# The second attention's first turn made beside the mixture's last batch

## The reference

```
# layer 0, second half: a dense mixture of 8 experts
probs = softmax(x1 @ gate_w + gate_b)
h = relu(einsum('bsd,edf->bsef', x1, w1) + b1)
moe = einsum('bse,bsed->bsd', probs, einsum('bsef,efd->bsed', h, w2) + b2)
x = x + memory(xn) + layernorm(x1 + moe)             # the sum of layer 0
xn = layernorm(x)
# layer 1
qkv = xn @ Wqkv.T + b                                # 16 heads of 8
ctx = causal_attention(q, k, v)
q2 = conv1d(ctx); out = causal_attention(q2, k, v) @ out_w.T
# and, beside it, 32 routed experts, top 8 of a router on xn, with capacity 128
x = x + out + routed(xn)
```

## Time and profile before

| | |
|---|---|
| three runs | 3534.44 us median, 3531.47 to 3535.82 |
| profiled execution, its time | 3539.05 us |
| its span, first to last instruction | 3537.2 us |
| mean granted TensorE clock | 0.968 of full |
| busy PE, DVE, ACT, POOL | 91%, 73%, 59%, 24% of the span |
| DMA | 151.89 MB, mean 43 GB/s |

### The profile page before, as it was taken

The page is one execution under the profiler, slowest core; times in us unless marked ns, Lnnn a source line. Parts: engine busy times, 40 slices in busy tenths (PEclk is TensorE's granted clock), DMA queues, the critical chain, the costliest instruction groups (busy, mean ns, idle before and its releaser), DMA issues. The chain is left out here.

```text
span 3537.2 us, 77376 instructions
## 1 busy us (share of the span) xinstructions
PE 3225.2 (91%) x30347; PEld 1871.8 (53%) x30347; DVE 2574.1 (73%) x5108; ACT 2070.9 (59%) x4201; POOL 832.5 (24%) x753
## 2 busy tenths in 40 slices
PE   6887699999999899999999999779999999999998
PEld 6876222222222377777777777535555444444454
DVE  5876788888888366766766766588777777777774
ACT  6774277777777543433433434237667767677776
POOL 3321111110110224323324324123333121111110
PEclk9998699999999999999999999879999999999999
DMA  4100211111111000110100100133222121111111
GB/s 140 31 13 1 61 46 55 55 46 46 52 47 37 26 19 24 35 31 23 38 30 23 38 29 23 29 81 68 59 61 49 48 65 48 44 46 53 42 28 28
DMA packets 180473, 151.89 MB, mean 43 GB/s; under 512 B 44388, under 2 KB 160900, under 8 KB 179972
## 3 DMA queue, kind: packets, MB, share of 16 engines
q1 hardware_dynamic: 172228, 140.43, 14.0%
q0 software_dynamic: 6144, 4.72, 1.0%
q10 hardware_dynamic: 1728, 1.57, 0.2%
HBM read 48.45 MB, written 32.65 MB: 23 GB/s over the span
## 5 line engine op out<-in xcount | busy, mean ns | idle before, releaser
L1409 DVE TENSOR_REDUCE b_maxima<-psum 128x2 f32<-128x1024 f32 (+3 forms) x768 | 773.4, 1045 | 216.8 <-PE psum L1241 208.7
L1347 ACT ACTIVATE b_prob<-psum 128x512 f32<-128x512 f32 (+2 forms) x1536 | 725.2, 525 | 316.7 <-PE psum L1274 304.2
L1409 DVE TENSOR_REDUCE c_maxima<-psum 128x2 f32<-128x1024 f32 x512 | 602.7, 1221 | 117.4 <-PE psum L1235 116.3
L1347 ACT ACTIVATE c_prob<-psum 128x512 f32<-128x512 f32 x1024 | 536.0, 601 | 194.0 <-PE psum L1267 194.0
L2081 PEld LDWEIGHTS psum<-consts_layer,a_hid 128*128 128x128 f32 x4096 | 476.2, 192 | 53.6 <-issue 53.3
L2071 PE MATMUL psum<-a_x1t,consts_layer 128*128 128x512 f32 x1024 | 463.7, 598 | 15.4 <-issue 9.9
L2081 PE MATMUL psum<-consts_layer,a_hid 128*128 128x128 f32 x4096 | 477.8, 274 | 0.0
L2138 ACT ACTIVATE a_hid<-psum,consts_layer 128x512 f32<-128x512 f32 x512 | 348.2, 687 | 213.5 <-PE psum L2071 207.4
L1267 PE MATMUL psum<-b_qa,b_ka 64*128 64x512 bf16 (+3 forms) x2048 | 359.5, 302 | 54.6 <-ACT b_prob L1347 52.1
L1289 PE MATMUL psum<-b_prob,b_v 128*32 128x512 f32 (+3 forms) x4096 | 385.8, 449 | 0.2
L2283 DVE SCALAR_TENSOR_TENSOR a_acc<-psum,a_gprob,a_acc 128x128 f32<-128x128 f32 x512 | 143.8, 343 | 286.5 <-PE psum L2081 274.5
(11 more groups left out here) (399 smaller groups left out, 4327.7 us busy)
## 6 DMA issues: line engine op xcount, KB each, us to landing
b_qa<-b_part SPq DMA_DIRECT2D x192, 128.0 KB
c_qa<-c_part SPq DMA_DIRECT2D x96, 128.0 KB, 2.4
c_ka<-c_part SPq DMA_DIRECT2D x90, 128.0 KB, 2.4
b_ka<-b_part SPq DMA_DIRECT2D x90, 128.0 KB
consts_layer<-layer_in SPq DMA_DIRECT2D x1, 5419.0 KB, 18.8
c_xt<-xnt SPq DMA_DIRECT2D x17, 256.0 KB, 2.8
m_xin<-x SPq DMA_DIRECT2D x16, 256.0 KB, 4.2
xnt<-m_xt SPq DMA_DIRECT2D x16, 256.0 KB, 2.8
```

Of the source, the lines that this page charges most:

```text
L1347: self.nc.scalar.activation(out, src, ACT.Exp, scale=SCALE).then_inc(self.s.free, 1)
L1409: self.nc.vector.reduce_max(out, src, X).then_inc(self.m.free, 1)
```

## The change

The second attention's turn -2 is taken out of `layer1` and made inside `mixture`, by a new class `Front`. It owns the attention's buffers for rows, parts and the first value buffer (placed on the other side of SBUF; the rest are allocated as before by `late`). Its pieces go to these places:

- SP: the loads of x for batches 0 and 1 before the last batch's experts (`after`); the cover and one fills of turn 0's buffers at expert 3; the six query rows at `behind` step 6 of the last batch, ahead of the store of `wts`. The load of x for batch 2 is the first thing that SP issues in `layer1`.
- GpSimd: tables, covers and the first value buffer before the last batch's experts; the other three value buffers stay in `layer1`.
- VectorE: the seven clears behind the accumulations of experts 2 to 5 of the last batch (`CLEARED`); the split and the bias of v at `behind` step 4, before the wait for the router.
- TensorE: q and k of batch 0 into banks 0 and 1 behind the last expert, then v once ScalarE has copied both.
- ScalarE: those copies behind the last expert; the six key rows at `behind` step 4, after the router's exponential.

`layer1` then begins with turn -1. The buffer `cover` becomes a view of `part[0]`.

```diff
+class Front:
+    QUERIES, KEYS, VALUES = 0, 4, 8
+    def sync_loads(self, sp):
+        self.load_x(sp, 0)
+        self.load_x(sp, 1)
+    def tensor_projection(self, pe):
+        nc, xt = self.nc, self.xt[0]
+        pe.wait_ge(self.x_loaded[0], 16)
+        for k, name in enumerate(("q1", "k1")):
+            nc.tensor.matmul(self.att.bank[k], self.K(name), xt[:, :], start=True, stop=True).then_inc(self.projected, 1)
+    def tensor_values(self, pe):
+        nc, att, xt = self.nc, self.att, self.xt[0]
+        pe.wait_ge(self.copied, 2)
+        for t in range(T):
+            last = nc.tensor.matmul(att.m.bank("v", 0)[:, 0, t * P:(t + 1) * P], xt[:, t * P:(t + 1) * P], self.K("v1"), start=True, stop=True)
+        last.then_inc(att.m.ready, 1)
+    def scalar(self, act):
+        nc, att, cols = self.nc, self.att, self.K("cols1")
+        for k in range(2):
+            act.wait_ge(self.projected, k + 1)
+            nc.scalar.activation(att.qk[:, k, :], att.bank[k], ACT.Identity, bias=cols[:, k:k + 1]).then_inc(self.copied, 1)
+    def vector_parts(self, dve):
+        dve.wait_ge(self.att.covers_ready, 5)
+        dve.wait_ge(self.copied, 2)
+        self.att.vector_first()
...
 # steps, at the end
             after()
             experts(NB - 1, 1, lambda e: behind(NB - 2, 0, e))
+            done()
             for e in range(E0):
                 behind(NB - 1, 1, e)
 # SP
                     if e == 6:
+                        if is_last(m):
+                            front.att.sync_parts(sp, 0)
                         made(sp, wts_ready, m)
...
+                        if is_last(m) and e == 3:
+                            front.att.sync_fresh(sp, 0)
+                def after():
+                    made(sp, xt2_stored, NB - 3)
+                    front.sync_loads(sp)
 # TensorE
+                def done():
+                    made(pe, my_copied, NB - 1)
+                    front.tensor_projection(pe)
+                    front.tensor_values(pe)
 # ScalarE, behind, step 4
                         nc.scalar.activation(rl[:, :, :], rl[:, :, :], ACT.Exp).then_inc(rexp_ready.sem, 1)
+                        if is_last(m):
+                            front.att.scalar_rows(act)
 # GpSimd, after
+                    made(pool, xn2_ready, NB - 2)
+                    front.pool_setup(pool)
 # VectorE, behind, step 4
+                        if is_last(m):
+                            front.vector_parts(dve)
+                            front.vector_values(dve)
                         made(dve, route_ready, m)
 # VectorE, experts
                         between(e)
+                        if is_last(m) and e in CLEARED:
+                            front.att.vector_clear(front.att.fresh[CLEARED[e]])
+CLEARED = {2: slice(0, 2), 3: slice(2, 4), 4: slice(4, 5), 5: slice(5, 7)}
 # layer1
-                load_x(0)
-                load_x(1)
-                for p in range(-2, len(turns) + 1):
+                sp.wait_ge(att.m.ready, att.m.count("v", 0))
+                front.load_x(sp, 2)
+                for p in range(-1, len(turns) + 1):
```

More of the change, by code:

```diff
@@ L1027, in __init__ @@
         self.ka = [sb(f"ka{n}", [P, H // 2, S], BF16) for n in range(n_keys)]
-        self.v = [sb(f"v{n}", [P, T, GAP + H * 32]) for n in range(n_keys)]
+        self.v = [sb("v0", [P, T, GAP + H * 32])]
         self.one = sb("one", [2, S], BF16)
[L1030 to L1035, removed]
         if causal:
@@ L1107, in heads, with plan @@
         return range(2) if self.together(s) else range(2 * u, 2 * u + 2)
-    def plan(self, more_m, more_s):
-        for p in range(-2, len(self.turns) + 1):
+    def plan(self, more_m, more_s, turns):
+        for p in turns:
             for s in range(SLOTS):
@@ L1933, in made_before, with steps @@
                 engine.wait_ge(signal.sem, signal.at(m - ago, signal.per))
-        def steps(engine, ahead, experts, behind, looped=lambda i: None, after=lambda: None, early=lambda m: None):
+        def steps(engine, ahead, experts, behind, looped=lambda i: None, after=lambda: None, early=lambda m: None, done=lambda: None):
             early(1)
@@ L1995, in experts @@
                         between(e)
-                steps(sp, ahead, experts, behind, early=early)
+                        if is_last(m) and e == 3:
[3 more added lines that the diff above has]
+                    front.sync_loads(sp)
+                steps(sp, ahead, experts, behind, early=early, after=after)
                 sp.wait_ge(zero_stored.sem, 32)
@@ L2091, in experts @@
                         between(e)
-                steps(pe, ahead, experts, behind)
+                def done():
+                    made(pe, my_copied, NB - 1)
+                    front.tensor_projection(pe)
+                    front.tensor_values(pe)
+                steps(pe, ahead, experts, behind, done=done)
             @block.scalar
@@ L2145, in experts @@
                         between(e)
-                steps(act, ahead, experts, behind)
+                steps(act, ahead, experts, behind, done=lambda: front.scalar(act))
             @block.gpsimd
@@ L2688, in _ @@
                         sp.wait_ge(att.m.ready, att.m.count("v", turns[p + 2].batch))
[L2689 removed]
+                        front.load_x(sp, turns[p + 2].batch + 2)
                     if att.has(p + 1):
@@ L2827, in extra @@
                     routed.vector(dve, p, s, own)
-                att.vector_clear(att.fresh[:att.cleared(0)])
-                for p in range(-2, len(turns) + 1):
+                for p in range(-1, len(turns) + 1):
                     att.vector_turn(dve, p, own, extra)
```

118 lines of the change are left out of this document (73 added, 45 removed).

## The result

| | median | lowest to highest | runs |
|---|---|---|---|
| before | 3535.65 us | 3531.47 to 3538.82 | 5 |
| changed | 3517.10 us | 3514.94 to 3522.48 | 5 |

The ratio is 0.9950, with a 95% interval from 0.9937 to 0.9963: faster by 0.5%, 18.6 us, where 3515.0 us and a gain of 19.4 had been predicted. The profiled execution of the changed kernel took 3518.61 us, with a span of 3516.7 and a mean granted clock of 0.972.

A forecast was written before the change was run, and what follows sets the result against it. A latency chain across the barrier between mixture and second attention was taken as the bound; first maxima moving from 2312.89 to 2293.5 gave 19.4 us, so 3534.44 became 3515.0 us, range 3510 to 3521.

The forecast's parts named there:

- main case: Second attention's start: first maxima 19.4 us earlier, everything behind shifting rigidly, to 3515.0 us; chance 0.50.
- Projection: q, k and v matmuls behind the last expert: at most 4.5 us for q, k and copies, hidden by VectorE's normalising.
- Split: VectorE's split of q and k in its router wait: 3.95 us, 3.81 covered, router 0.8 us late.
- Rows: Twelve row transfers: landing 9.14 us after first issue, plus 0.3 for the store and 0.1 for starting; maxima at 2293.5.
- Clears: Seven VectorE buffer clears, 14.9 us, between accumulations of experts 2 to 5: cost nothing, with 1.6 us or more to spare.
- GpSimd: 11.2 us of setup moved into its idle time; free at about 2300, first split at 2304.8, covered with 4 us spare.
- Barrier: At the mixture's end: opens 2.3 us after the weights' store is issued, at 2291.0, ahead of the rows.
- rival A: Weights' store completes only with the rows, opening the barrier up to 2.3 us later: gain 17.5, 3516.9 us; chance 0.14.
- Rival B: Rows land late, 7.33 us after the last key row's issue: gain 15.6, 3518.8 us; chance 0.12.
- Rival C: TensorE's raised clock in turn -1 falls elsewhere: lost, 3518.2 us (0.07), or won, 3512.0 us (0.12); chance 0.19 in all.
- D: No change: something behind turn -1 that doesn't move swallows the shift, 3534 us; chance 0.03.
- E: Clears and GpSimd's setup stretch the last experts by up to 26.1 us: 6.7 us slower, 3541 us; chance 0.02.

The follow-up runs named there:

- e5: Changed kernel, with VectorE's split and values' addition behind the router's weights and SP's query rows behind their store; 3550.14 us, ratio 0.9976 to the kernel before.
- e2: Changed kernel, with the barrier no longer waiting for the last store of the router's weights; 3520.47 us, ratio 0.9956 to the kernel before.
- e4: As e3, with ScalarE's six key rows issued ahead of the router's exponential; 3519.34 us, ratio 0.9953 to the kernel before.
- e6: Changed kernel, with five of the seven clears moved behind the last accumulation (expert 7); 3552.90 us, ratio 0.9986 to the kernel before.
- e7: Changed kernel, with each of the seven clears made twice at its place; 3552.16 us, ratio 0.9981 to the kernel before.
- e3: As e2, with SP's load of x for batch 2 and three fills held until the rows landed; 3519.70 us, ratio 0.9951 to the kernel before.
- f3: Kernel before the change, with GpSimd's clears of value buffers 1 to 3 held until the twelve rows landed; 3562.89 us, one execution.
- f1: Kernel before the change, with SP's next load of x and the fills held until the twelve rows landed; 3565.14 us, one execution.

## Why the prediction was right

**The main case** held in its structure: every instruction came where it was put, TensorE took none of the moved work on the path and VectorE 0.55 us of it, and the rest shifted rigidly (32.06 us against the 32.0 forecast). The time lies 2.1 us above the forecast, inside the range. Read from T, the maxima came 18.85 us nearer, where 19.4 had been forecast: 0.45 of the difference is the store. That the medians' 18.6 us agree so well with 18.85 is partly luck, since the two traces' difference holds some 1.9 us of slow rows (below).

**Projection.** 1.88 us for q and k at their new place, where "at most" the old 4.5 had been allowed for projection and copies; 2264.11 to the end of the second copy at 2266.72 is 2.6. Hidden, as forecast.

**Split.** From T to its end 3.85 us (forecast 3.97), the router 0.55 late (forecast 0.8). `e5` shows its worth: 7.4 us.

**Rows.** Forecast 9.14 us and 0.3 for the store; measured 9.75 in `e2` and 9.81 and 9.87 with nothing behind the rows. With the store out of the way the maxima come at T + 13.62, where the forecast was T + 13.54. The step "ScalarE's late start should cost little" held: `e4` finds nothing.

**Clears.** They cost nothing, as forecast: 33.87 and 33.88 us. `e6` gives the price without cover, 2.13 each. But the cover was judged too simply, though it made no difference here. I read it from VectorE's waits alone, "1.6 us to spare or more". VectorE's idle time left before the accumulations is 2.20, 2.26, 3.57 and 1.37 us, about as worked out, yet `e7` shows that what runs out next is ScalarE's exponential, queued ahead of the next relu.

**GpSimd.** Its first split came at 2302.89, 11.21 us behind the first maxima, after 4.71 us of idle time (forecast 4): covered.

**The step that failed** is *Barrier*: "2288.7 + 2.3 = 2291.0, ahead of the rows". The store was issued at 2285.83, and the barrier opened at 2291.2, 5.4 us later. The 2.28 us of a store that goes alone don't hold for one queued behind rows. The barrier came 0.45 us behind the rows instead of ahead of them, and so set the start. This is the mechanism of **rival A** (0.14). Its condition came true, its price was mis-sized: 17.5 had been worked out for its gain, with up to 2.3 us behind the rows, where `e2` measures 0.45; that its 3516.9 is the forecast nearest to 3517.1 is no proof of that size. The prediction had the reason in its own sentence on A and gave it too little weight. The store's time to landing, from all transfers of `table` between 2260 and 2345, minimum, median, maximum:

```profile
DMA to landing us min/median/max: 1.8/2.2/4.9
```

The 4.9 is this store, 64 KB behind 1.57 MB of rows. The packet records say where its extra 3.1 us lie. Alone, in the old trace, its first packet moved 0.90 us after the issue (2288.55), the last one 0.46 later, and its signal was complete 0.42 after that. Here its first packet moved 3.27 us after the issue, at 2289.10, right behind the last query row of the same queue of SP (2288.94); it then took 0.81 and 0.80 us. So 2.4 us pass while it waits behind the rows of SP's own queue, which share the engines with ScalarE's, and 0.7 go to moving and signalling beside ScalarE's key rows. The Trainium skill, DMA: Bandwidth & Descriptors, section on queues, rings and completion order, says that the increment lands only after every earlier write of that DMA engine, whichever queue it came from. The trace allows that, since the store's signals came from 2290.37 on and the key rows' last packet ended at 2290.29, but what the rule can have added is only the signalling's 0.4 us, not 3.1.

**Rival B**, late landing, is refuted in its cause: its 7.33 us were put down to the x load and the fills, and `e2`, `e3` and `f3` show that these cost nothing. From the last key row the same step takes 6.21 us in `f1` and 6.30 in `f3`; what lengthened it in the earlier trace rows was most likely the code packet. **Rival C**, the clock, did not happen as a loss or a gain. The raised stretch did wander, as these windows of the changed kernel show:

```profile
2291.60:2303.50 11.90, 9.62 (x70) 3.99 (x70) 7.94 (x8) 1.37 (x2) 6.96 (x12) 0.52 0.27 47
2304.00:2306.50 2.50, 1.32 (x30) 0.88 (x30) 2.50 (x4) 0.00 (x0) 2.43 (x2) 0.99 0.00 0
2306.90:2323.70 16.80, 13.53 (x138) 9.74 (x139) 12.28 (x16) 0.38 (x2) 2.46 (x2) 0.50 0.41 112
```

TensorE was granted 0.99 (2.4 GHz) from 12 us behind the first maxima; before it was 19 us behind them. In that stretch VectorE is busy 2.50 of 2.50 us and TensorE 1.32: the reductions pace it, so a fast TensorE brings nothing. Before, the fast stretch lay mostly over 32 matmuls of one column (`L2401`, 2332.20, 3.68 us); here the same ones (`L2505`, 2311.04) run at half clock and take 3.68 us too. The stretch from maxima to scores was 31.87 to 32.23 in the nine kernels with the change or a part of it, wherever the clock rose. **D** is refuted by the rigid shift. **E** is refuted at this size, though `e7` shows that its first half is there: with the clears doubled TensorE falls behind, and it costs 9.6 us.

**A size from one execution.** Of the 18.85 us that the two traces show, some 1.9 seem to be the old execution's slow rows, 11.80 us against 9.9. The sum used them rightly, against that execution's own 3539.05 us, but then carried the gain over to the median unchanged, though that execution stood 4.6 us above it. The trace held the hint: 4.76 and 5.00 us of issue against 3.85 and 4.10 for the same six rows in the first attention, where no code packet lay beside them.

## What to carry over

A chain that crosses a barrier is shortened by starting its second half in the last wait ahead of the barrier, but what is then queued ahead of the last store decides when the barrier opens: price that store by what is in flight, not by its time alone, or let only its reader wait for it. Cover for a moved step is the idle time of its engine only as long as no other engine waits in order for a result behind it; follow that result to the queues that it releases. Where one execution shows the same instructions slower than elsewhere in the same trace, look whether a code packet moved beside them, and price the gain with and without it, since the median may hold less of it.

## What the runs showed of the hardware

- **A small store lands with the large transfers ahead of it.** 64 KB took 4.9 us to land behind twelve transfers of 128 KB, 1.8 at shortest elsewhere; 2.4 of the 3.1 us more passed before its first packet moved, behind the six that stood in its own queue.
- **Code is loaded through the same DMA engines.** One packet of 16384 bytes lasts 0.9 to 1.7 us in the stretches read here. Row transfers beside one took up to 2.37 us to issue instead of at most 0.87, and a set of twelve up to 8.96 us instead of 7.32.
- **Two engines, two queues, one rate.** With both queues started together or 1.2 us apart, the same twelve transfers took 9.87 and 9.81 us. Moving data while VectorE or GpSimd clears buffers cost them nothing (9.89 to 9.94 us with the clears, 9.95 without).
- **GpSimd is held by some operations of VectorE and not by others.** The cast of `b_kmask` (128x64) takes 1.31 us before, where it lies beside VectorE's subtraction of 128x1024 (2299.84 to 2301.08), and 0.23 us at its new place, where VectorE was in none:

```profile
2234.64 1.03 POOL L1154 TENSOR_TENSOR b_covers<-b_covers,consts_layer 16x512 bf16<-16x512 bf16 x1
2235.62 0.52 POOL L1156 CAST b_pick<-consts_layer 128x128 bf16<-128x128 f32 x2
2236.09 0.23 POOL L1157 CAST b_qmask<-consts_layer 128x64 bf16<-128x64 f32 x1
2236.27 0.23 POOL L1158 CAST b_kmask<-consts_layer 128x64 bf16<-128x64 f32 x1
```

The product for `b_covers` at 2234.64 lies inside a clear of VectorE (2234.27 to 2236.03) and is not longer for it, nor is the clear: 1.76 us everywhere. The Trainium skill, SBUF — State Buffer, section on the two separate sides, has the pair of ports shared by VectorE and GpSimd as an exclusive lock. The section names what takes the lock on VectorE's side: an operation in a two-port mode, or one with two SBUF inputs beside a GpSimd operation that reads SBUF. The trace agrees: the subtraction has two inputs, and the memsets, which read nothing, show no lock. Rival E left this condition out; its fear had no ground for these clears.
